# The last units of a one-core attention and expert kernel: statistics over three units, the shift on POOL, norms two blocks at a time, splits and turns apart, a third weights buffer, the Silu table load moved

## What is computed

```
mod = silu(c) @ wmod                       # six vectors: sa ca ga sb cb gb
h = layernorm(x) * (1 + ca) + sa
x = x + ga * attention(h)                  # 16 heads, softmax over 2048 positions, head width 64
h = layernorm(x) * (1 + cb) + sb
x = x + gb * (shared(h) + routed(h))       # 8 experts, the best 2 of each token, silu(h w1) * (h w3) @ w2
```

## Time and profile before

| | |
|---|---|
| runs, us | 1307.74, 1302.77, 1306.95; median 1306.95 |
| profiled execution, us | 1303.49, its span 1301.6 |
| mean granted TensorE clock | 0.993 of 2.4 GHz |
| PE busy | 1273.1 us, 98% of the span |
| POOL busy | 1103.5 us, 85% |
| DVE busy | 991.4 us, 76% |
| ACT busy | 905.6 us, 70% |

### The profile page before, as it was taken

How to read it: one execution, slowest core, us unless ns; L and a number is a source line. 1 busy time by engine, 2 the same in 40 slices (tenths; PEclk the granted TensorE clock), 3 DMA queues, 4 the chain that set the end, 5 groups by cost and what they waited for, 6 DMA issues and landing times. The chain is left out here.

```text
span 1301.6 us, 22469 instructions
## 1 busy us (share of the span) xinstructions
PE 1273.1 (98%) x8604; PEld 692.1 (53%) x8604; DVE 991.4 (76%) x1253; ACT 905.6 (70%) x1127; POOL 1103.5 (85%) x507
## 2 busy tenths in 40 slices
PE   7899999999999999999999999999999999999998
PEld 5454555555554545555554545555555545445787
DVE  5677778877777778787777777787878777878675
ACT  6576767686777767676767777676767677785474
POOL 2299989898989999898989899998989898998544
PEclk9899999999999999999999999999999999999999
DMA  8020202011010202020110202020200102001323
GB/s 212 1 49 10 58 10 58 9 36 26 15 50 10 58 9 58 10 57 10 26 33 10 58 9 58 9 58 9 58 10 9 49 9 58 9 10 42 98 73 90
DMA packets 39948, 49.82 MB, mean 38 GB/s; under 512 B 8570, under 2 KB 19202, under 8 KB 39842
## 3 DMA queue, kind: packets, MB, share of 16 engines
q1 hardware_dynamic: 39698, 48.39, 14.4%
q10 hardware_dynamic: 144, 0.00, 0.0%
HBM read 21.83 MB, written 1.24 MB: 18 GB/s over the span
## 5 line engine op out<-in xcount | busy, mean ns | idle before, releaser
L963 ACT ACTIVATE probs<-ps 128x1024 f32<-128x1024 f32 x512 | 498.5, 1031 | 49.5 <-PE ps L1421 42.4
L1439 PE MATMUL ps<-probs,v_sb 128*64 128x512 f32 x2048 | 514.2, 606 | 0.0
L1053 POOL TENSOR_TENSOR acc<-acc,probs 128x1024 f32<-128x1024 f32 x192 | 459.4, 2393 | 56.9 <-ACT probs L963 55.2
L1124 DVE TENSOR_REDUCE peak_parts<-ps 128x2 f32<-128x1024 f32 x297 | 360.5, 1218 | 138.0 <-PE ps L1369 137.1
L1053 POOL TENSOR_TENSOR acc_odd<-acc_odd,probs 128x1024 f32<-128x1024 f32 x192 | 458.9, 2390 | 0.0
L900 ACT COPY peak_copy<-ps 128x1024 f32<-128x1024 f32 x215 | 218.5, 1016 | 226.6 <-PE ps L1369 131.4
L1138 DVE TENSOR_REDUCE peak_parts<-peak_copy 128x2 f32<-128x1024 f32 x215 | 260.5, 1212 | 34.6 <-ACT peak_copy L900 34.1
L1439 PEld LDWEIGHTS ps<-probs,v_sb 128*64 128x64 f32 x2048 | 121.8, 136 | 174.4 <-issue 129.1
L1415 PE MATMUL ps<-q_hi,d_hi 64*128 64x512 f32 x512 | 202.3, 395 | 1.3 <-ACT probs L963 1.3
L1415 PE MATMUL ps<-q_hi,d_swap_hi 64*128 64x512 f32 x512 | 202.2, 395 | 0.4 <-ACT probs L963 0.4
L1421 PE MATMUL ps<-q_hi,d_lo 64*128 64x512 f32 x512 | 200.5, 392 | 0.0
(11 more groups left out here) (245 smaller groups left out, 1607.2 us busy)
## 6 DMA issues: line engine op xcount, KB each, us to landing
k_swap_hi<-k_hi SPq DMA_DIRECT2D x64, 128.0 KB, 2.3
d_swap_hi<-d_hi SPq DMA_DIRECT2D x64, 128.0 KB, 2.4
d_swap_lo<-d_lo SPq DMA_DIRECT2D x64, 128.0 KB, 2.3
acc_odd<-sums_dram SPq DMA_DIRECT2D x62, 128.0 KB, 2.9
shifts<-peakT SPq DMA_DIRECT2D x256, 0.5 KB
q_hi<-weights_dram SPq DMA_DIRECT2D x8, 256.0 KB, 3.5
q_lo<-weights_dram SPq DMA_DIRECT2D x8, 256.0 KB, 4.3
k_hi<-weights_dram SPq DMA_DIRECT2D x8, 256.0 KB, 5.8
```

Source lines behind the costliest of these rows:

```text
L963: act.activation(probs[:, kt % PROBS, :], ps[:, 2 * place:2 * place + 2, :].rearrange("p a b -> p (a b)"), ACT.Exp, scale=SCALE).then_inc( ...
L1053: pool.tensor_tensor(total, total, probs[:, kt % PROBS, :], ALU.add).then_inc(added, 1)
L1124: dve.tensor_reduce(peak_parts[:, :, i // STRETCHES, i % STRETCHES], ps[:, bank:bank + 2, :], AX.X, ALU.max).then_inc(peak_free, 1)
L1439: mm = pe.matmul(ps[at:at + HEAD_DIM, PV_BANK, :], v_sb[:, p, chunk_of(kt) * HEAD_DIM:(chunk_of(kt) + 1) * HEAD_DIM], probs[:, kt % PROBS, ...
```

## The change

The same instructions on the same data as before, apart from two small operations that move from DVE to POOL and one added ACTIVATE of one column. What moves:

- `stats` 0, 1 and 2 go from places 18, 20 and 22 of unit 29 to place 20 of units 25, 27 and 29.
- `root` goes from place 25 to place 24, `rstd` from 28 to 26. The two operations of the shift go from DVE to POOL, behind its twelfth add of unit 29.
- `norm` runs in six groups of two blocks at places 2 to 22 of unit 30, and no longer in three groups of four at 2, 10 and 14.
- `turn` 0, 1, 2 and the thirds of `split w1` stand at single places from 26 of unit 30 to 2 of unit 31. `logits` goes from place 3 to 6 of unit 31, `gate` from 4 to 7.
- The thirds of `split w3` stand at 17, 18 and 21; `weights` 2 at 23 and no longer at 19 beside 0 and 1. It has a buffer of its own, the second half of `wqT`.
- An ACTIVATE with Silu on one column stands ahead of the last `copy_pv`, so the table load stands there too.

```diff
-BEFORE_LAST_PLACES = {18: [("stats", 0)], 20: [("stats", 1)], 22: [("stats", 2)], 25: [("root", 0)], 28: [("rstd", 0)]}
+STATS_PLACE = 20
+BEFORE_LAST_PLACES = {24: [("root", 0)], 26: [("rstd", 0)], 27: [("shift", 0)]}
 LAST_HEAD_PLACES = (
-    {2: [("norm", 0)], 10: [("norm", 1)], 14: [("norm", 2)],
-     27: [("turn", 0), ("turn", 1)],
-     28: [("split w1", 0), ("split w1", 1), ("split w1", 2)], 31: [("turn", 2), ("left", 0), ("left", 1)]},
-    {2: [("left", 2)], 3: [("logits", 0)], 4: [("gate", 0)],
-     17: [("split w3", 0), ("split w3", 1), ("split w3", 2)], 19: [("weights", 0), ("weights", 1), ("weights", 2)]},
+    {2: [("norm", 0)], 6: [("norm", 1)], 10: [("norm", 2)], 14: [("norm", 3)], 18: [("norm", 4)], 22: [("norm", 5)],
+     26: [("turn", 0)], 27: [("split w1", 0)], 30: [("turn", 1)], 31: [("split w1", 1)]},
+    {1: [("split w1", 2)], 2: [("turn", 2)], 3: [("left", 0), ("left", 1), ("left", 2)], 6: [("logits", 0)], 7: [("gate", 0)],
+     17: [("split w3", 0)], 18: [("split w3", 1)], 19: [("weights", 0), ("weights", 1)], 21: [("split w3", 2)],
+     23: [("weights", 2)]},
 )
...
+    if stats is not None:
+        places[STATS_PLACE].append(("stats", stats))
...
+        STATS_HEADS = range(HEADS - 4, HEADS - 1)
+        SHIFT_AFTER = 12
...
+                                     stats=STATS_HEADS.index(t * 2 + p) if half == 1 and t * 2 + p in STATS_HEADS else None)
...
-        weightT = [w[0:EXPERTS, 0:BANK] for w in (wqT, wkT)]
+        weightT = [wqT[0:EXPERTS, 0:BANK], wkT[0:EXPERTS, 0:BANK], wqT[0:EXPERTS, BANK:2 * BANK], wkT[0:EXPERTS, 0:BANK]]
...
-                if i >= 2:
-                    act.wait_ge(weights_out, 16 * (i - 1))
-                act.copy(weightT[i % 2], job.ps[0:EXPERTS, :]).then_inc(tail_free, 1)
+                if i == 3:
+                    act.wait_ge(weights_out, 16 * 2)
+                act.copy(weightT[i], job.ps[0:EXPERTS, :]).then_inc(tail_free, 1)
...
+        def early_shifts(pool):
+            at = slice(0, READY_BLOCKS)
+            pool.wait_ge(early_rstd, 1)
+            pool.tensor_tensor(shift_ln[:, at], mean_var[:, at, 0], rstd[:, at], ALU.mult).then_inc(early_shift, 1)
+            pool.wait_ge(early_shift, 1)
+            pool.tensor_scalar(shift_ln[:, at], shift_ln[:, at], -1.0, None, ALU.mult).then_inc(shift_ln_ready, 1)
...
-                                    norm_act(act, range(4 * i, 4 * i + 4), 2)
+                                    norm_act(act, range(2 * i, 2 * i + 2), 2)
...
             pairs_of_heads(body)
+            act.activation(std[:, 0:1], eps[:, :], ACT.Silu)
             copy_pv(UNITS)
...
                         add(unit, half, n)
+                        if n == SHIFT_AFTER and any(kind == "shift" for s in plan for pl in s for kind, _ in pl):
+                            early_shifts(pool)
...
-                                    shifts_of(dve, link, range(READY_BLOCKS), 3)
+                                    dve.wait_ge(std_ready, 3)
+                                    dve.reciprocal(rstd[:, 0:READY_BLOCKS], std[:, 0:READY_BLOCKS]).then_inc(early_rstd, 1)
```

More of the change, by code:

```diff
@@ L83, in chunk_of, with side_jobs @@
     return half * 8 + pair * 2 + odd
-def side_jobs(half, sums=True, outs=True, project=True, pairs=True, early=True, last_head=False, before_last=False):
+def side_jobs(half, sums=True, outs=True, project=True, pairs=True, early=True, last_head=False, before_last=False, stats=None):
     places = [[] for _ in range(4 * PAIRS)]
@@ L292, in units @@
                                      pairs=not (final_head and half == 1), early=not final_head,
-                                     last_head=final_head, before_last=last and p == 0 and half == 1)
+                                     last_head=final_head, before_last=last and p == 0 and half == 1,
+                                     stats=STATS_HEADS.index(t * 2 + p) if half == 1 and t * 2 + p in STATS_HEADS else None)
                     yield p, half, t * 2 + p, t * 4 + (2 * p + half), plan
@@ L445, in build @@
         weight_nat = small[:, 6]
-        weightT = [w[0:EXPERTS, 0:BANK] for w in (wqT, wkT)]
+        weightT = [wqT[0:EXPERTS, 0:BANK], wkT[0:EXPERTS, 0:BANK], wqT[0:EXPERTS, BANK:2 * BANK], wkT[0:EXPERTS, 0:BANK]]
         weights_dram = nc.dram_tensor("weights_dram", [EXPERTS, TOKENS], F32, kind="Internal").ap()
         weights_ready = sem("weights_ready")
+        early_rstd, early_shift = sem("early_rstd"), sem("early_shift")
         weights_out = sem("weights_out")
@@ L720, in spread_weights @@
             sp.wait_ge(tail_free, tail("weights", g).full)
-            sp.dma_start(weights_dram[:, g * BANK:(g + 1) * BANK], weightT[g % 2]).then_inc(weights_out, 16)
+            sp.dma_start(weights_dram[:, g * BANK:(g + 1) * BANK], weightT[g]).then_inc(weights_out, 16)
             sp.wait_ge(weights_out, 16 * (g + 1))
```

## The result

| | before | changed |
|---|---|---|
| runs shared in time, us | 1301.27 to 1310.92, median 1306.39 (14) | 1296.78 to 1301.55, median 1298.06 (14) |
| profiled execution, us | 1303.49, span 1301.6 | 1296.78, span 1294.7 |
| mean granted clock | 0.993 | 0.997 |

The ratio of the means is 0.9944, 95% interval 0.9929 to 0.996: 7.3 us faster (the medians are 8.3 apart), where 4.5 were summed and 1301 was forecast. The time is inside the range. The gain, 0.56%, stands at the border between the likeliest outcome (within 0.5%) and faster. The spread of the runs halves, from 9.6 to 4.8 us, which the prediction did not foresee.

A forecast was written before the change was run, and what follows sets the result against it. The prediction took PE, busy for 98% of the span, as the bound. Terms of 4.9 us less 0.4 gave 4.5 won: 1299.0 from the profiled execution, 1302.5 from the median, forecast about 1301, range 1295.5 to 1305.5.

The forecast's parts named there:

- unit 29, statistics and shift, less root: Unit 29: PE's waits of 1.55 and 1.25 us for DVE go, the root costs 1.3, so 1.5 us won.
- unit 30, norms by two: Unit 30: smaller norm groups on ACT let the copy that frees PE's pair come in time, 0.8 us won.
- `turn` and split apart: Ahead of tile 15's exponential: standing apart, the two fit, and PE's wait goes, 0.4 us won.
- third weights: Unit 31: with a third buffer ACT's copy no longer waits for a DMA; PE's waits go, 1.6 us won.
- low clock: Unit 31, behind the logits: one 1.2 GHz stretch stays, so 0; bounds 1.7 us won (chance 0.15) or lost (0.1).
- gate: Unit 31: DVE's gate moves behind other work and is late for PE by 0.4 us, bounds 0 to 7.
- Silu table: Table load moves to ACT's idle time ahead of the last copy; PE's wait goes, 0.6 us won.
- POOL at the end: POOL's last add before PE's sum: its cover of 2.0 us shrinks, so 0.2 us may come back.
- the new wait of unit 29: Unit 29: PE waits about 1.1 us for ACT's exponential ahead of tile 15, as the root stands earlier.
- One of its own signs of being wrong: From 1094 to 1211: the prediction is wrong if PE's waits still sum to more than 3 us.
- That rival: Unit 29, ACT: table switches cost load and drain, about 2.66 us each; 2.8 us less won, about 1304, chance 0.03.
- The rival: Unit 31: gate comes late, PE stands ahead of the weights' transposition; up to 7 us, 1305.6, chance 0.15.

The follow-up runs named there:

- e1: The kernel before with the unit 29 part alone (statistics over three units, root, `rstd`, shift on POOL): 1303.32 us, ratio 0.9972.
- e8: The changed kernel with the norms in three groups of four at places 2, 10 and 14 as before: one run, 1297.54 us.
- e6: The changed kernel with the end as before (all weights at place 19, two buffers, no early table load): 1305.08 us, ratio 0.9995 to the kernel before.
- e3: The changed kernel with the square root back at place 25: 1298.31 us, ratio 0.9931 to the kernel before.
- e7: The changed kernel with DVE's jobs for the sums of unit 29 spread apart in unit 30: 1299.28 us, ratio 0.9941 to the kernel before.
- e2: The kernel before with only the logits moved from place 3 to 6 and the gate from 4 to 7 of unit 31: 1308.27 us, ratio 1.0012.
- e4: The changed kernel with the last sum one expert item later: 1297.39 us, ratio 0.9931 to the kernel before.
- e5: The kernel before with the end alone (third weights buffer, `split w3` thirds and third weights copy at own places, early Silu table load): 1301.9 us, ratio 0.997.
- e9: The kernel before once more, unchanged, for its profile: one execution, 1311.33 us.
- e11: The kernel before with one edit, the shift's two operations on POOL behind its twelfth add of unit 29: 1304.13 us, ratio 0.9975.
- e10: The changed kernel with root at 25, last sums one item later, unit 30's sum jobs apart, weights places later: 1296.58 us, ratio 0.9926 to the kernel before.

## Why the prediction was right

| term | summed | measured in the profiles |
|---|---|---|
| unit 29, statistics and shift, less root | 1.5 | 1.57 (e1: 1.55), and 0.5 more in unit 30 |
| unit 30, norms by two | 0.8 | 0 |
| `turn` and split apart | 0.4 | 0.42 |
| third weights | 1.6 | 1.29 + 0.29 waits gone |
| low clock | 0 | 1.7 |
| gate | -0.4 | 0 |
| Silu table | 0.6 | 0.6 |
| POOL at the end | -0.2 at most | -1.35 |

In the profiled execution unit 29, the `turn`, the third weights and the Silu table came out as summed, and the new wait of unit 29 where and as large as worked out. That the sum's 4.5 stands near the 5.2 us of the profile is partly luck. Two terms failed, the norms by 0.8 us and POOL's add by 1.15. The clock (1.7), the gate (0.4) and the 0.5 us in unit 30 made up for them. One of its own signs of being wrong came true, PE's waits, which sum to 3.1 us, just over the 3 named. Of what it said the changed profile would show, the end of the waits for the copy in unit 30 did not come. The forecast of 1301 was 2.9 us above the median. The two switches of ACT's table cost 1.28 us each and no drain, as in the rows above: the root starts 0.02 us behind its load. That rival is out.

**The norms, 0.8, failed.** The prediction took the group of norms for what delays the copy because it stands in front of it on ACT. The copy's own releaser was not read: it is DVE's L1157. e8 shows it, and ACT's 0.90 us of idle time ahead of the copy says the same.

**POOL's last add was sized too small**, 0.2 against 1.35. The cover of 2.0 us was right. PE came to the sum 8.0 us earlier (1216.46 against 1209.78 - 1.35), POOL began its last add only 5.15 earlier, and that add took 2.70 instead of 2.40. Both sizes were a little off. POOL restarts in unit 31 at 1182.91 before and at 1177.54 in the changed kernel; from there PE wins 2.66 us (2.2 were counted), and POOL's thirteen operations take 32.09 us and not 31.57. With the 2.0 of cover that makes 1.2 of the 1.35.

**The gate was in time**, with 0.8 us to spare and not 0.4 late. It starts 3.6 us later inside the unit, where 4 and a sum of 1.2 were counted, and PE comes 1.4 earlier, where 0.4 was counted. The 0.63 us that the prediction calls a split operation alone is the first of three beside POOL's adds; all three take 1.28 us in e6. The rival was real one step on: with unit 29 1.4 us shorter (e3), and in e7 with the sums' jobs moved, PE waits 1.5 to 1.6 there. In both the gate's first operation met an add of POOL and took 1.61 and 2.43 us, not 0.19.

**The low clock** is absent from the profile, 1.7 us won within its stated bound, by the luck of the execution, as e2 and e4 show.

**What the sum could not see** is that its execution was a short one. The shift's price on DVE was taken as 4.05 us and the wait behind it as 1.25. In half of the profiles (e5, e9) it is 6.3 and 3.5, with some 1.7 us of low clock behind. For the third copy's wait, 3.37 on ACT and 1.29 on PE, the other profiles with all weights at one place have 4.12 to 5.97 and 2.04 to 3.88. So both terms were right for the profile and too small for the median. e11 (3.3 us against 1.25 summed) and e5 (about 3.9 against 2.2) measure them. Whether the halved spread comes from here is not shown: e11 and e5 spread over 5.8 and 6.4 us, but e1, with the shift on POOL, over 7.0 and e2, with it on DVE, over 4.5. The start of unit 29 alone differs by 3.7 us between five profiles.

The terms are not additive. e1 and e5 sum to 7.6 us, near the whole; but e6, which has all but the end, gains 0.7 where e1, with less, gains 3.7. Their intervals just overlap. What stays open is how much of e6's loss is the interplay and how much the execution's chance, and whether the copy's later place alone would do.

## What to carry to other kernels

Read the releaser of the late instruction itself before blaming what stands in front of it. Where a wait ends at a transfer whose time another engine sets, gains upstream stop there until the instruction that waits stands later in its queue; a second buffer may add little to that. Take the profiled execution's place among the runs seriously: when runs spread by more than the sum, look for the step whose price varies, since removing it is worth its mean, not the price in one profile.

## What the runs showed of the hardware

- **Long PE waits cost more than their length.** The granted clock fell to its lower level of 1.2 GHz right behind each of six such waits (3.88 in e1, 3.57 in e5, 3.51 in e6, 3.54 and 3.82 in e9, 3.67 in e11) and behind one of 2.04 (e2), for about 3.4 us in most, which is 1.7 us more lost, and for twice that in e11. Behind the waits of 1.35 to 1.58 us in the rows above it stayed full. Behind the 2.85 us of logits, with no wait, it fell in seven of the fourteen profiles and stayed full in seven.
- **A DVE operation on SBUF beside POOL's adds has no fixed price.** The same three remainders (two of 128x384, one of 128x256) took 1.28 us (e6), 3.48 (changed), 4.35 (e11), 6.53 (before) and 14.56 (e3, of the w1 split). A 128x12 operation took 1.76 or 4.05. I had read the rows as "until the add in hand is over". It can last over one whole add more, and in e10 a single 128x384 operation lasted 9.56 us. It began 0.3 us behind the start of an add and ended 0.4 us behind the end of the fourth, when POOL paused:

```profile
1156.81 9.56 DVE L1277 TENSOR_TENSOR w_lo<-w1T,k_hi 128x384 fp32r<-128x384 f32 x1 [3.17 <-ACT k_hi L1001]
...
1156.50 2.44 POOL L1072 TENSOR_TENSOR acc<-acc,probs 128x1024 f32<-128x1024 f32 x1
...
1163.50 2.45 POOL L1072 TENSOR_TENSOR acc_odd<-acc_odd,probs 128x1024 f32<-128x1024 f32 x1
```

- **Two small operations on POOL between two adds** took 0.21 and 0.26 us, and 0.20 to 0.26 in all ten profiles that have them there.
